# Idle matmuls in the first and the last graph's waits of TensorE, in a four-layer graph network kernel

## The reference, cut to what matters

```
h = relu(layernorm(x)); x = x + attention_8_heads(h, adj)      # layer 0
h = relu(layernorm(x)); x = x + gated_attention(h, adj)        # layer 1
h = relu(layernorm(x)); x = x + gru_5_times(h, adj)            # layer 2
h = relu(layernorm(x)); x = x + conv17_distance_gru(h)         # layer 3
```

```
m = h @ weight[l];  agg = A.T @ m
r, z = sigmoid(...agg..., ...h...);  n = tanh(i_n + r * h_n)
h = (1 - z) * n + z * h
```

## Time and profile before

| | us |
|---|---|
| median of 3 runs | 2175.18 |
| lowest and highest | 2172.43, 2176.92 |
| profiled execution | 2177.26 |
| its span, first to last instruction | 2175.2 |
| TensorE busy | 2061.6 (95%) |
| VectorE busy | 1609.2 (74%) |
| ScalarE busy | 1517.9 (70%) |
| GpSimd busy | 777.0 (36%) |
| mean granted clock of TensorE, as a share of the full one | 0.986 |

### The profile page before, as it was taken

How to read it: one execution, slowest core, us unless ns; L and a number is a source line. 1 busy time by engine, 2 the same in 40 slices (tenths; PEclk the granted TensorE clock), 3 DMA queues, 4 the chain that set the end, 5 groups by cost and what they waited for, 6 DMA issues and landing times. The chain is left out here.

```text
span 2175.2 us, 36465 instructions
## 1 busy us (share of the span) xinstructions
PE 2061.6 (95%) x12700; PEld 1748.4 (80%) x12700; DVE 1609.2 (74%) x4782; ACT 1517.9 (70%) x2968; POOL 777.0 (36%) x888
## 2 busy tenths in 40 slices
PE   7799999999999999999999999999999999999876
PEld 6678797887978878797887979888797888879754
DVE  5687887868778687887868778686877868788643
ACT  5677594967849677694967859587694967859432
POOL 2334334242423433333343433434243342433311
PEclk9999999999999999999999999999999999999988
DMA  3101001010100101001010100101001010100100
GB/s 120 49 20 45 25 1 44 26 45 25 45 25 2 44 25 45 25 2 50 19 45 25 45 25 2 44 25 45 25 28 42 1 44 25 45 6 1 49 0 5
DMA packets 47319, 65.73 MB, mean 30 GB/s; under 512 B 3744, under 2 KB 21536, under 8 KB 47008
## 3 DMA queue, kind: packets, MB, share of 16 engines
q1 hardware_dynamic: 47136, 63.41, 8.9%
HBM read 59.21 MB, written 4.19 MB: 29 GB/s over the span
## 5 line engine op out<-in xcount | busy, mean ns | idle before, releaser
L644 PE MATMUL banks<-F,PT 128*128 128x128 f32 x4096 | 543.3, 276 | 2.3 <-DVE PT L1223 1.5
L644 PEld LDWEIGHTS banks<-F,PT 128*128 128x128 f32 x4096 | 507.1, 192 | 15.2 <-DVE PT L1223 2.0
L478 POOL TENSOR_TENSOR HS<-HT,HS 128x512 fp32r<-128x512 f32 x64 | 83.4, 1304 | 539.4 <-ACT HS L990 539.4
L1223 DVE COPY PT<-banks 128x512 f32<-128x512 f32 x256 | 175.7, 686 | 116.2 <-PE banks L638 115.5
L926 ACT ACTIVATE PT<-banks 128x512 f32<-128x512 f32 x256 | 151.2, 591 | 89.0 <-PE banks L638 87.1
L961 ACT ACTIVATE F<-banks,dcols 128x512 f32<-128x512 f32 x288 | 193.6, 684 | 23.3 <-PE banks L512 19.1
L445 POOL TENSOR_SCALAR tiles<-tiles,rden 128x512 f32<-128x512 f32 x192 | 143.7, 763 | 97.1 <-DVE rden L1213 96.9
L415 POOL TENSOR_TENSOR rstd<-var,mhalf 128x4 f32<-128x4 f32 x64 | 72.4, 1131 | 271.4 <-DVE var L1126 271.4
L508 PE MATMUL banks<-HS,WH 128*128 128x512 f32 (+1 forms) x368 | 157.9, 429 | 1.6 <-ACT HS L889 1.4
L445 POOL TENSOR_SCALAR U<-U,rden 128x512 f32<-128x512 f32 x192 | 130.5, 699 | 72.7 <-DVE rden L1213 72.5
L509 PE MATMUL banks<-HS,WLO 128*128 128x512 f32 (+1 forms) x368 | 147.5, 401 | 0.0
(11 more groups left out here) (216 smaller groups left out, 5309.3 us busy)
## 6 DMA issues: line engine op xcount, KB each, us to landing
adjN<-in_adj_dram SPq DMA_DIRECT2D x32, 1024.0 KB, 5.6
adjT<-in_adjt_dram SPq DMA_DIRECT2D x16, 1024.0 KB, 5.7
xin<-in_x_dram SPq DMA_DIRECT2D x18, 256.0 KB, 2.9
out_dram<-X SPq DMA_DIRECT2D x16, 256.0 KB, 6.0
F<-in_wraw_dram SPq DMA_DIRECT2D x1, 1076.0 KB, 9.6
adjT<-in_c2w_dram SPq DMA_DIRECT2D x1, 1024.0 KB, 11.1
PT<-in_fcw_dram SPq DMA_DIRECT2D x1, 512.0 KB, 5.2
PT<-in_fpw_dram SPq DMA_DIRECT2D x1, 512.0 KB, 6.8
```

The costliest lines, as they stand in the source:

```text
L478: pool.tensor_tensor(HL[s], HT[s][:, :], HH[s].bitcast(F32), ALU.subtract).then_inc(S["h_new_low"], 1)
L644: last = pe.matmul(B[s][:, 3, part(j)], PT[s][:, k, part(j)], G[s][:, k, h * DIM:(h + 1) * DIM], start=(h == 0 and j == 0 and k == 0), sto ...
L1223: dve.tensor_copy(PT[s][:, j, :], pt_bank(s, j)).then_inc(S["pt_dve"], 1)
```

## The change

A helper `busy(bank, n)` issues n matmuls of WH's first 128 columns as weights with its first 512 columns as the moving operand into a bank whose old content is no longer needed. Nothing reads the result. It is called at six places. In graph 0 the wait for `raw_low` moves ahead of the transposes with it.

```diff
+            def busy(bank, n):
+                for k in range(n):
+                    pe.matmul(bank, WH[:, 0:P], WH[:, 0:4 * P])
 ... layer1
                 yield
-                transpose_in(g, 1)
-                yield
-                pe.wait_ge(*own("h_high", g, 1))
                 if g == 0:
                     pe.wait_ge(raw_low, 1)
+                    busy(B[s][:, 1, :], 18)
+                transpose_in(g, 1)
+                yield
+                pe.wait_ge(*own("h_high", g, 1))
 ... layer1, its end
                 yield
+                if g == GRAPHS - 1:
+                    busy(B[s][:, 1, :], 24)
                 transpose_in(g, 2)
 ... layer2, cells 2 to 5
                     else:
+                        if g == GRAPHS - 1:
+                            pe.wait_ge(*after("r", cell - 1))
+                            busy(B[s][:, 2, :], 10)
                         pe.wait_ge(*after("h_new", cell - 1))
 ... layer3
                 yield
+                if g == GRAPHS - 1:
+                    pe.wait_ge(*after("r", cell - 1))
+                    busy(B[s][:, 2, :], 10)
                 pe.wait_ge(*after("h_new", cell - 1))
                 transpose_out(g, HT[s])
                 yield
+                if g == GRAPHS - 1:
+                    busy(B[s][:, 2, :], 13)
                 transpose_in(g, 3)
 ... layer3, ahead of the gates of the last cell
                 yield
+                if g == GRAPHS - 1:
+                    pe.wait_ge(*after("c2_scaled", g))
+                    busy(B[s][:, 3, :], 13)
                 pe.wait_ge(*after("nmp_low", g))
```

More of the change, by code:

```diff
@@ L682, in layer1 @@
                 yield
+                if g == 0:
+                    pe.wait_ge(raw_low, 1)
+                    busy(B[s][:, 1, :], 18)
                 transpose_in(g, 1)
@@ L685, in layer1 @@
                 pe.wait_ge(*own("h_high", g, 1))
-                if g == 0:
-                    pe.wait_ge(raw_low, 1)
                 high(B[s][:, 2, :], W("WA"), (HH[s], HL[s]))
```

## The result

The changed kernel takes 2170.88 us (median of 20 runs, 2169.41 to 2173.33) against 2174.87 us before (20 runs, 2172.43 to 2177.67). The ratio is 0.9982, with a 95% interval of 0.9976 to 0.9989: 4.0 us less, between 2.4 and 5.2. The profiled execution took 2170.93 us with a span of 2168.9 us; before it was 2177.26 and 2175.2.

A forecast was written before the change was run, and what follows sets the result against it. TensorE bounds nine tenths at full clock; the last graph's chain has waits where its clock falls. Terms -5.02, -2.3, -0.2, +2.44 and 0 sum to -5.1, from median 2175.2: 2170.1, said as 2169.9 us, range 2166.5 to 2174.0.

The forecast's parts named there:

- Cells 2 to 5, -5.02 us: Last graph: ten idle matmuls in each 3.37 us wait keep the clock full, each cell 10.40 us; gain 5.02 us.
- The hole ahead of cell 1, 0: Last graph: 24 idle matmuls leave 2.0 us of 7.66 empty, the clock falls, cell 1 keeps its 1.24 us; gain 0.
- the rule on transposes: Trainium skill: full clock does not engage for transposes; hole ahead of cell 1 then nearly 5 us, otherwise 2.0 us.
- The entry of layer 3, -2.3 us: Last graph: 13 idle matmuls in 4.22 us speed transposes, matmuls and first taps; gain 2.3 us, lower bound 0.47 us.
- the second rival: Clock also falls at layer 3's entry and first graph, or earlier timed runs had fewer falls: 2172.1 us, chance 0.29.
- The 13 ahead of the gates, +2.44 us: Last cell: 13 idle matmuls in a 0.65 us wait start the gates' matmuls 2.44 us late; clock already full.
- The first graph, -0.2 us: 18 idle matmuls in a 5.26 us wait: gain 0.2 us taken, lower bound 0, upper bound 1.8 us.
- The last transposes, 0: End of last graph: 4.33 us wait without idle matmuls, transposes stay at 1.12 us; at best they save 0.47 us.
- Faster by over 0.2%, 0.65: Whole kernel: measured time below 2170.8 us; chance 0.65, from the forecast and the first rival.
- the case called the same: Whole kernel: time neither below 2170.8 us nor above 2179.5 us; chance 0.29, from the second rival.
- The third rival: Idle matmuls don't count for the clock, or too few do: +5.1 to +6 us, 2180.7 us, chance 0.06.
- The first rival: The clock holds in every hole: -6.7 us, 2168.4 us, chance 0.15.

The follow-up runs named there:

- the filled versions: The change without the 13 ahead of the gates, holes filled nearly to the end: 2168.13 us; the same with none in the first graph: 2167.19 us.

## Why the prediction was right, and where its sizes were off

- **Cells 2 to 5, -5.02 us.** The two profiles differ by 5.04 us there, the three other profiles without the tens by 4.8 to 4.9, and the tens alone, which also shorten layer 3's first transposes, gave 5.4 us (3.5 to 7.4). Right.
- **The hole ahead of cell 1, 0.** Right that the clock falls: it did so at this place in all five profiles that have the 24 with a hole of 2.2 us behind them. The cell takes 11.59 to 11.96 us in them, where 11.64 was assumed. That the waits ahead of it were the reason is shown by the filled versions: with 0.4 and 0.2 us left of 2.2 and 0.69, cell 1 takes 10.39 or 10.40 us. That the first of the two did it, as the prediction argued from graph 4's, isn't shown. The prediction's rows had one reading wrong, without effect on this: VectorE's time in cell 1 is 5.78 us, not about 5.1, and the cell takes 10.4 us at full clock all the same. The sentences that weighed the rule on transposes called the fall certain by it. The fall is there, but the rule isn't needed for it, since the transposes between the cells held the clock in the profile.
- **The entry of layer 3, -2.3 us.** 1.68 us in the stretch to the first tap and 0.63 us in the taps: 2.31. Right, and the clock held over 1.22 to 1.25 and 0.69 us of waits in all four profiles of the change and of it without the gates' 13. So the second rival's first half didn't come.
- **The 13 ahead of the gates, +2.44 us.** 2.42 us in the profile, 3.3 us (1.3 to 5.2) for them alone, 2.8 us side by side. Right, and it takes back over a third of what the others give. Two small errors in it cancel: the 13 took 3.25 us, not 3.05, but behind them the second real matmul follows the first after 0.24 us, where before it followed after 0.51. The chain has 17 matmuls to the end of the gates, not 18; the sum doesn't use their number.
- **The first graph, -0.2 us.** 0.0003 above 1 within 0.0009: nothing to be seen. The bound from below was the case, for the reason given with it: the clock falls behind the 18. The bound from above was too high: it counts 0.58 us for the first transposes, which take 1.10 us at full clock because VectorE's tiles pace them, as the prediction itself says of cell 1.
- **The last transposes, 0.** 1.11 us at the end of the changed kernel, as before. The saving of 0.47 us at best is what the 14 in the filled version took. That they stay slow isn't certain, though: they took 0.66 us after the same 4.33 us of waiting, with nothing to fill it, in the profiles with only tens or transposes between the cells.
- **The sum, -5.1, made 2169.9 us; measured 2170.88, -4.0.** The last graph's stretches sum to -4.75 in the profiles, near the forecast of -5.1. The step that was off is the last, from the profile to the median. The two profiled executions differ by 6.33 us, of which 1.55 lie ahead of the last graph's stretch; the other 4.8 us are 0.8 more than the medians show. I took the sum's 5.1 us from the median whole, and then 0.2 more because the scatter should shrink; in these 20 runs each it hardly did (standard deviation 1.4 us before and 1.2 after), in the later ones side by side it did (1.6 and 0.8). The second rival's second half, that the timed runs before had fewer falls than the profiled one, has the runs on its side. Of the 73 later runs of the kernel before, the eight with a mean clock of 0.990 took 2171.6 to 2172.9 us, the 14 with 0.985 or 0.986 took 2175.9 to 2178.6. The profiled execution, 2177.26 us at 0.986, belongs to the slower ones; 45 of the 73 were at 0.987 or 0.988. And the profile with the first graph's 18 alone, whose last graph is the kernel before's, has 115.35 us from graph 14's last transposes to the end of the span, where the kernel before has 116.1 and the changed one 111.35: 4.0 us. It stays an argument, since 4.8 and 5.1 us both lie in the interval of 2.4 to 5.2 us.
- **Faster by over 0.2%, 0.65.** The median lies 0.18% below, 0.36 us short of that bound. So the case called the same, which I gave 0.29, is what happened by that bound, though the kernel is faster beyond its interval.
- **The third rival**, idle matmuls that don't count: out, by every profile with ten idle matmuls between the cells (10.4 us for each of cells 2 to 5).
- **The first rival**, a clock that holds in every hole: not in any profile of the change. By its own terms its time is 2168.5 us, not 2168.4.

## What to carry to other kernels

Where one chain alternates between TensorE and other engines, look at the clock in each window of it: a hole of 3.4 us cost 1.1 to 2.3 us in the work behind it, most of the time, and matmuls that nobody reads removed this where they filled the hole to about 1 us. That isn't a bound that holds everywhere: in the first graph the clock fell behind waits of 1.21 and 0.37 us. Give each place its count from its own hole: ten in 3.37 us were free, 13 in 0.65 us cost 2.4 us in the profile and bought nothing, since the clock was full there. A place whose remaining hole is 2 us is half done. Filling the small rests took 1.8 us off the last graph in the profiles (108.8 to 107.0), and 1.2 and 1.4 us off the medians, which the scatter doesn't let one tell from nothing.

## What was not expected of the hardware

- Float32 transposes of 128x128 kept the full clock in the profiled execution: 20 of them in 2.35 us in a hole of 3.4 us, PEclk 1.00 in all four cells.
- In the first graph the fall was put off and not avoided, whatever was filled. There the low clock ended between 102 and 104 us before (PEclk 0.71 in that window) and between 104 and 106 in the changed kernel (0.56), and in the version with the first graph's holes filled it began only at 104 us, behind waits of 1.21 and 0.37 us. None of the first graph's idle matmuls gained anything that the runs show.
- The same hole of 3.37 us was followed by a fall in some cells and not in others, within one execution and between executions. The runs of the kernel before scatter with their mean clock, from 2171.69 us at 0.990 to 2178.36 at 0.985 among 24. Not all of the scatter is the last graph's: graph 14's last transposes start anywhere in 2.6 us, and the changed kernel's 20 runs still spread over 3.9 us.
